# Attention on one core: one exponential over three score tiles, two score tiles ahead of each group's products, and the identity bias in 32-column array tiles

## What is computed

```python
x = x + attention(layernorm(x))
x = x + ffn(layernorm(x))
# attention, for each batch b of 4 and head h of 16
scores = q @ k.T / sqrt(8) + bias[h]      # (1024, 1024)
weights = softmax(scores)
out = weights @ v                          # (1024, 8)
out = concat(heads) @ w_gate + b_gate; a, g = split(out); return a * sigmoid(g)
```

## Time and profile before

| | us |
|---|---|
| three runs | 669.5, 670.9, 678.7 |
| median | 670.9 |
| the profiled execution | 669.6 |
| its span, first to last instruction | 667.8 |
| attention loop, first score tile to last copy | about 71 to 565 |

### The profile page before, as it was taken

One profiled execution on the slowest core, in us unless ns is written; L12 is line 12 of the kernel. 1 busy time (PEld: TensorE's weight loads), 2 busy tenths in 40 slices (PEclk: granted clock), 3 DMA queues, 4 the chain that ended last, 5 costly groups with the idle time before them and its releaser, 6 DMA issues.

```text
span 667.8 us, 12697 instructions
## 1 busy us (share of the span) xinstructions
PE 606.4 (91%) x4011; PEld 166.2 (25%) x4011; DVE 566.7 (85%) x691; ACT 548.4 (82%) x599; POOL 105.8 (16%) x95
## 2 busy tenths in 40 slices
PE   6892699999999999999999999999999998599775
PEld 2441122222222222222222222222222222234432
DVE  5973599999999999999999999999999996114776
ACT  2862599999999999999999999999999997011353
POOL 5740600010110101010110101010101101013412
PEclk8897599999999999999999999999999999855855
DMA  9136460525335261615244351615153401500004
GB/s 211 65 95 140 137 135 18 134 50 106 76 79 114 48 131 26 137 37 125 62 93 94 64 123 36 134 25 133 45 117 65 89 9 22 147 8 0 0 1 126
DMA packets 30175, 54.44 MB, mean 82 GB/s; under 512 B 9561, under 2 KB 21214, under 8 KB 29022
## 3 DMA queue, kind: packets, MB, share of 16 engines
q1 hardware_dynamic: 29870, 53.97, 36.0%
q10 hardware_dynamic: 288, 0.26, 0.1%
HBM read 43.86 MB, written 9.18 MB: 79 GB/s over the span
## 4 chain that ended last, share of the span: by engine, by line
ACT 37%; issue 31%; PE 11%; DVE 5%; DMA 3%; ACTq 1%; POOL 1%; DVEq 0%; SPq 0%
ACT pbuf L969 16%; ACT split L969 15%; PE ps L1151 4%; ACT pbuf L977 3%; PE ps L892 3%; ACT split L977 2%; PE ps L867 2%; DMA rd<-r_scratch 2%; DVE kb L1372 1%; PE ps L1153 1%; DVE split L1367 1%; PE ps L876 1%; ACTq L968 1%; PE ps L1165 1%; ACT o_sbs L733 1%
## 5 line engine op out<-in xcount | busy, mean ns | idle before, releaser
L926 DVE TENSOR_TENSOR pbuf<-ps,t 128x1024 f32<-128x1024 f32 x192 | 232.5, 1223 | 20.0 <-PE ps L867 15.4
L926 DVE TENSOR_TENSOR split<-ps,t 128x1024 f32<-128x1024 f32 x192 | 229.4, 1217 | 12.9 <-PE ps L867 7.3
L969 ACT ACTIVATE pbuf<-pbuf 128x1024 f32<-128x1024 f32 x192 | 207.2, 1260 | 19.8 <-DVE pbuf L926 19.6
L867 PE MATMUL ps<-qb,kb 64*128 64x512 f16 x1024 | 184.0, 390 | 22.1 <-SPq L793 14.8
L969 ACT ACTIVATE split<-split 128x1024 f32<-128x1024 f32 x192 | 202.5, 1268 | 1.1 <-DVE split L926 1.0
L892 PE MATMUL ps<-pbuf,vst 128*32 128x512 f32 x1024 | 137.2, 608 | 0.0
L892 PE MATMUL ps<-split,vst 128*32 128x512 f32 x1024 | 136.0, 604 | 1.0 <-ACT split L977 1.0
L867 PEld LDWEIGHTS ps<-qb,kb 64*128 64x128 f16 x1024 | 48.4, 93 | 308.7 <-DVE pbuf L926 113.9
L876 PE MATMUL ps<-t64s,ident 128*64 128x512 f16 x512 | 80.6, 395 | 0.0
L977 ACT ACTIVATE split<-ps 128x1024 f32<-128x1024 f32 x64 | 78.6, 1228 | 0.0
L977 ACT ACTIVATE pbuf<-ps 128x1024 f32<-128x1024 f32 x64 | 78.2, 1222 | 0.0
(11 more groups left out here) (134 smaller groups left out, 359.1 us busy)
## 6 DMA issues: line engine op xcount, KB each, us to landing
t<-g_scratch SPq DMA_DIRECT2D x16, 960.0 KB
kb<-k_scratch SPq DMA_DIRECT2D x120, 64.0 KB
t64s<-gh_scratch SPq DMA_DIRECT2D x16, 248.0 KB
t64s<-gl_scratch SPq DMA_DIRECT2D x16, 248.0 KB
qb<-q_scratch SPq DMA_DIRECT2D x60, 64.0 KB
x_sb<-in_L_attn_x SPq DMA_DIRECT2D x4, 512.0 KB, 7.6
q_scratch<-split SPq DMA_DIRECT2D x8, 256.0 KB, 3.4
k_scratch<-split SPq DMA_DIRECT2D x8, 256.0 KB, 3.7
```

The source lines that it names most:

```text
L867: last = eng.matmul(ps[:, u + c, :], kb[p][rows, keys], qb[p][rows, b * HALF:(b + 1) * HALF], start=True, stop=True)
L926: eng.tensor_tensor(slot(g, b), banks(unit(k), 2), t128[p][:, t * P:t * P + S], ALU.add).then_inc(z_ready, 1)
L969: eng.activation(buf, buf, ACT.Exp).then_inc(p_ready, 1)
```

## The change

It does three things in the attention loop.

- ScalarE does batches 0 to 2 of a group in a single exponential over 3072 adjacent columns (`slots`), and it does the PSUM tile of batch 3 first. A semaphore `pd_ready` of its own counts the PSUM exponentials; `p_ready` now counts the wide ones.
- TensorE issues score tiles 0 and 1 of group g + 2, then the identity products of group g + 1, then products half 0 of g, score tile 2, products half 1, score tile 3. The identity products have become a function of their own, `bias(i, g)`, and stand a group later than the scores that they add to.
- The identity products are eight matmuls with 32 output columns in place of four with 64, so they use the same shape of array tile as the products. The band is loaded 32 columns wider.

VectorE's code is not touched. ScalarE's copy of half 1 stands between the PSUM exponential and the wide one of group 1.

```diff
@@ sizes
-T64W = 2 * S - 64
+T64W = 2 * S - 32
@@ in scores: batch 3 waits for the PSUM exponential alone
-                            eng.wait_ge(p_ready, i * (8 * GPH) + 4 * g)
+                            eng.wait_ge(pd_ready, i * (2 * GPH) + g)
@@ the identity products
-                    for c in range(2):
-                        for m in range(2):
-                            c0 = t * P + 64 * m + c * HALF
-                            last = eng.matmul(ps[64 * m:64 * m + 64, u + c, :], ident2[:, :],
+                def bias(i, g):
+
+                    p, t = (g // GPH) % 2, g % GPH
+                    for c in range(2):
+                        for m in range(4):
+                            c0 = t * P + 32 * m + c * HALF
+                            last = eng.matmul(ps[32 * m:32 * m + 32, 4 + c, :], ident2[:, 0:32],
                                               t64[p][:, c0:c0 + HALF], start=False, stop=True,
                                               skip_group_check=True)
                     last.then_inc(sp_ready, 1)
@@ in products, half 0
-                        eng.wait_ge(p_ready, i * (8 * GPH) + 4 * (g + 1))
+                        eng.wait_ge(pd_ready, i * (2 * GPH) + (g + 1))
+                        eng.wait_ge(p_ready, i * (2 * GPH) + (g + 1))
@@ TensorE's list
-                        for steps, c in (((0,), 0), ((1,), 1), ((2, 3), None)):
...
-                                for b in steps:
-                                    scores(i, g + LAG, b)
...
-                            if c is not None:
-                                products(i, g, c)
+                        if g + LAG < 2 * GPH:
+                            scores(i, g + LAG, 0)
+                            scores(i, g + LAG, 1)
+                            bias(i, g + LAG - 1)
+                            products(i, g, 0)
+                            scores(i, g + LAG, 2)
+                            products(i, g, 1)
+                            scores(i, g + LAG, 3)
+                            continue
@@ ScalarE's list
-                        for b in range(B):
-                            buf = slot(g, b)
-                            if b < DPG:
-                                eng.wait_ge(z_ready, i * (2 * DPH) + (DPG * g + b + 1))
-                                eng.activation(buf, buf, ACT.Exp).then_inc(p_ready, 1)
...
-                                eng.activation(buf, banks(4, 2), ACT.Exp).then_inc(p_ready, 1)
+                        eng.wait_ge(sp_ready, i * (2 * GPH) + (g + 1))
+                        eng.wait_ge(groups_done, i * (2 * GPH) + (g + 1))
+                        eng.activation(slot(g, DPG), banks(4, 2), ACT.Exp).then_inc(pd_ready, 1)
...
+                            copy_half(eng, 0, 1).then_inc(o_ready[1], 1)
+                        eng.wait_ge(z_ready, i * (2 * DPH) + DPG * (g + 1))
+                        eng.activation(slots(g, DPG), slots(g, DPG), ACT.Exp).then_inc(p_ready, 1)
```

More of the change, by code:

```diff
@@ L725, in attention_block @@
         p_ready = sem("p_ready")
+        pd_ready = sem("pd_ready")
         GPH = TB
@@ L749, in slot, with slots @@
             return pbuf[:, n, :] if n < 8 else splitf[:, (n - 8) * S:(n - 7) * S]
+        def slots(g, n):
+            k = 4 * (g % SETS)
+            return big[:, k * S:(k + n) * S] if k < 8 else splitf[:, (k - 8) * S:(k - 8 + n) * S]
         def unit(k):
@@ L902, in _ @@
                         scores(0, g, b)
+                    if g < LAG - 1:
+                        bias(0, g)
                 with eng.Fori(0, NH2) as i:
                     for g in range(2 * GPH):
-                        for steps, c in (((0,), 0), ((1,), 1), ((2, 3), None)):
-                            if g < 2 * GPH - LAG:
-                                for b in steps:
-                                    scores(i, g + LAG, b)
[L910 to L914, removed]
-                            if c is not None:
-                                products(i, g, c)
+                        if g + LAG < 2 * GPH:
[7 more added lines that the diff above has]
+                            continue
+                        if g + LAG == 2 * GPH:
+                            with eng.If(i < NH2 - 1):
+                                scores(i, g + LAG, 0)
+                                scores(i, g + LAG, 1)
+                            bias(i, g + LAG - 1)
+                        else:
+                            with eng.If(i < NH2 - 1):
+                                scores(i, g + LAG, 0)
+                                scores(i, g + LAG, 1)
+                                bias(i, g + LAG - 1)
+                        products(i, g, 0)
+                        with eng.If(i < NH2 - 1):
+                            scores(i, g + LAG, 2)
+                        products(i, g, 1)
+                        with eng.If(i < NH2 - 1):
+                            scores(i, g + LAG, 3)
             @block.vector
@@ L964, in _ @@
                     for g in range(2 * GPH):
-                        for b in range(B):
-                            buf = slot(g, b)
-                            if b < DPG:
-                                eng.wait_ge(z_ready, i * (2 * DPH) + (DPG * g + b + 1))
-                                eng.activation(buf, buf, ACT.Exp).then_inc(p_ready, 1)
[L970 to L976, removed]
-                                eng.activation(buf, banks(4, 2), ACT.Exp).then_inc(p_ready, 1)
[L978 to L986, removed]
-                                copy_half(eng, 0, 1).then_inc(o_ready[1], 1)
@@ new lines, in _ @@
+                        if g == SETS // 2:
+                            eng.wait_ge(qk_out, 16 * 4 * B)
+                        eng.wait_ge(sp_ready, i * (2 * GPH) + (g + 1))
+                        eng.wait_ge(groups_done, i * (2 * GPH) + (g + 1))
+                        eng.activation(slot(g, DPG), banks(4, 2), ACT.Exp).then_inc(pd_ready, 1)
+                        if g == LAG - 1:
+                            with eng.If(i > 0):
+                                eng.wait_ge(groups_done, i * (2 * GPH) + SETS)
+                                eng.wait_ge(o_stored[1], i * (16 * B))
+                                copy_half(eng, 1, 1).then_inc(o_ready[1], 1)
@@ L988, in _ @@
+                        if g == GPH + LAG - 1:
+                            eng.wait_ge(groups_done, i * (2 * GPH) + (GPH + SETS))
+                            eng.wait_ge(o_stored[0], i * (16 * B) + 16 * B)
+                            copy_half(eng, 0, 1).then_inc(o_ready[1], 1)
+                        eng.wait_ge(z_ready, i * (2 * DPH) + DPG * (g + 1))
+                        eng.activation(slots(g, DPG), slots(g, DPG), ACT.Exp).then_inc(p_ready, 1)
                 eng.wait_ge(groups_done, H * GPH + SETS)
```

1 line of the change is left out of this document (removed).

## The result

The changed kernel takes 716.6 us (median of four runs, 712.6 to 718.6); the kernel before, measured beside it, 671.0. The ratio is 1.065, 95% interval 1.055 to 1.074. The forecast was 692, with a range of 683 to 705: the direction was right, the size was half of what came. The profiled execution took 717.3 with a span of 715.2, 47.4 more than before.

A forecast was written before the change was run, and what follows sets the result against it. ScalarE was taken to set the 3.75 us period, TensorE 0.02 behind. Period 3.2, head ends 17.1 and edges 1.1 and 0.7 add 22.1 to the profiled 669.6, 691.7; forecast 692, range 683 to 705.

The forecast's parts named there:

- rival A: Attention loop: engine work counts and waits hide, period falls to 3.57, 23 us less, 647; chance 5%.
- the chain over two groups: Products through identity products, PSUM and wide exponentials to products two groups later: 7.46 us, so period at least 3.73.
- score tile 1's wait for VectorE: Score tile 1 overwrites banks VectorE's third addition reads: starts at 4.05 instead of 3.95, period 3.78.
- VectorE's copy holding up two additions: Head's end: copy waits for products ahead of two additions, score tile 1 is 1.3 us late, 1.2 after slack.
- the edges: Loop's start and end: first products wait for one more addition, +1.1 us; last products come 3.57 after the previous, +0.7.
- The bias parts' loads: Head loads growing from 1984 to 2016 columns, 1.6%, under a 30 us head: priced at nothing.
- 1.14 at its end: Extra time at each of 15 head ends, from both copies' waits, less today's 0.48: +17.1 us in all.
- 0.03 in each of 8 groups: Mid-head period 3.78 against 3.75, over 128 groups: +3 to +4 us, taken as 3.2.
- gave back: Head's end: the gap after ScalarE's copy returns 0.16 us, since ScalarE is then fed early.
- B's shorter chain: No measurable change: exponential 2.58 and quicker notices, period 3.65, about 676; chance 12% including a cheaper-copies case at about 683.
- C's causes: Heavier: 32-column identity tiles run worse, or VectorE's pitch is 1.20; 5 to 14 us over forecast, 697 to 706; 13%.
- the assumption: TensorE's granted clock stays at its upper level of 1.00 in the loop; a fall at head ends wasn't excluded.

The follow-up runs named there:

- one_wait: Changed kernel without the products' wait for the PSUM exponential, leaving one semaphore: loop 532.3 us against 535.1, 31.98 to 32.08 between copies where no load is late.
- all_four_mended: Changed kernel with VectorE's copy behind the third addition, ScalarE's copy first, q loads earlier and one semaphore ahead of products: loop 495.1 us, total 672.4.
- q_loads_earlier: Changed kernel with the next head's four q loads issued ahead of the waits for the two copies: loop 523.6 us against 535.1, total 706.6.
- identity_64_columns: Changed kernel with the identity products as before, four of 64 columns: loop 532.6 us against 535.1, lowest between copies 32.23.

## Why the prediction was right and wrong

**Right, and shown.** Engine work shrank as worked out (wide exponential 2.76 for 2.77; eight identity products in two passes), and none of it arrived, for rival A's counter-argument: the chain over two groups. Its length is in the traces: no two successive periods of the loop, head's ends included, add to less than 7.55 in the changed kernel, where the prediction had 7.46. With a single semaphore ahead of the products the least is 7.46 (one_wait, all_four_mended), and with three exponentials, 2.94 for 2.76, it is 7.73. TensorE's old order makes the chain 0.2 shorter, so that it fits under TensorE's own work, and takes away score tile 1's wait for VectorE; the period falls to 3.72. VectorE's copy holding up two additions was the largest single item: moving it took 19 us off the loop, and the gap it makes was 4.99 for a forecast 4.98. At the edges the first products came 1.1 later, as forecast, and the last products came 3.56 after the ones before (600.74, 604.30), forecast 3.57.

**The step that failed most.** "The bias parts' loads grow from 1984 to 2016 columns, 1.6%, under a head that is 30 us long: nothing." The size was not the question. I compared the loads with a head's length, but they start only when both copies are done and are needed by the first score tile two groups before the head's end, which left 22.4 us in the kernel before; no row was read for how much of that they use. The change makes the copy that triggers them later and the tile that needs them earlier: 20.5 us are left between the two, 1.9 less, and the loads took up to 23.1. It cost 11.6 us of the profiled loop, shown by the q loads sent earlier and again by ScalarE's copy put first.

**Mis-sized terms.** Free of late loads, a head costs 1.81 more than before, where I had 1.14 at its end and 0.03 in each of 8 groups, 1.37 or so. Gap by gap between first products, in q_loads_earlier, the 0.44 lie behind ScalarE's copy (4.54 for 4.36) and in the five mid-head periods (3.99, 3.85, 3.71, 3.85 and 3.80, on average 3.84 in place of 3.78); the gap between the two gave back 0.05 more than forecast. One cause is shown: the start of the products after an exponential, taken from a row with one semaphore (0.05) though the diff gives them two (0.14), worth 0.27 a head by the one_wait run. Where the other 0.17 come from is open. The second half's products waiting 0.44 for ScalarE's copy are not it: with the copy put first that wait is gone, and only one gap fell, by 0.49, the copy's own slot.

**Chance.** 5.9 us of the profiled difference lie behind the loop, in the granted clock of unchanged code. What makes the clock fall there in some executions and not in others stays open. It doesn't explain the medians, which differ by 45.6. The mean granted clock was 0.907 in the profiled execution and 0.903 in q_loads_earlier, the two with some 109 us behind the loop, and 0.911 to 0.919 in the ten experiments with 102.7 to 104.6. The changed kernel's other three runs have 0.915 to 0.919 and still took 712.6, 715.9 and 718.6. With 71.1 ahead of the loop and some 103.4 behind it, an estimate from those traces, their loops took 536 to 542, more than the profiled 535.1. So the late loads probably cost more there than 11.6.

So the miss of 25.3 (47.4 less the forecast 22.1) is 11.6 of late loads, 6.6 of mis-sized terms (15 x 0.44), 5.9 behind the loop, and 1.2 that I can't place.

**The rivals.** A (the gain arrives) fell. B's shorter chain too: the exponential took 2.76, not 2.58, and the notices were slower. Of C's causes the first, 32-column tiles running worse, was tested twice and is nothing. The second, a VectorE pitch of 1.20, did occur, in two groups of a head: with the input ready an addition follows the last by 1.13 to 1.14, but where its score tile comes just before it by 1.23 or 1.30. The first of these two rows has such an addition, the second none:

```profile
281.75 3.66 DVE L952 TENSOR_TENSOR split<-ps,t 128x1024 f32<-128x1024 f32 x3 [0.90 <-PE ps L873]
...
297.22 3.49 DVE L952 TENSOR_TENSOR split<-ps,t 128x1024 f32<-128x1024 f32 x3 [0.36 <-PE ps L873]
```

No score tile waited behind either kind of late addition, so it cost nothing that shows. The loss beyond my range had another source.

Of the granted clock in the loop, the assumption held: 1.00 in every 100 us from 100 to 600, with idle pieces up to 2.6 us ahead of a head's first score tile.

## What to carry to other kernels

When an engine's list is strict, a wait that was free is priced by what stands behind it: before an instruction is moved on one engine, look for every rare instruction elsewhere (a copy once a head, a transfer's trigger) that waits for it, and for what is queued behind that one. A transfer hidden under a long stage has a start and a need of its own; read the distance between the two and how much of it is used, never the stage's length. And when work between a producer and its consumer is made coarser, add up the whole chain between them, over as many groups as it spans, and compare it with the busiest engine's own work over as many: three results handed over at once are fine where the chain stays below it (some 7.34 against 7.44) and useless where one score tile ahead of the identity products lifts it above (7.55).

## What the runs showed of the hardware

A second semaphore on the same instruction costs time even if it was reached long ago: products with two started 0.14 us after the exponential's end, with one 0.04 to 0.05. In the kernel before, a VectorE addition that also waits for a free buffer started 0.52 after its score tile's start, though a score matmul lasts 0.39; the additions that wait for their scores alone started 0.43 after. That is 0.13 against 0.04, but on VectorE no run took the second wait away.

A change of the array's shape costs about 0.10 us of TensorE: the last identity pass stood 0.22 ahead of the products in the same shape and 0.31 in another (identity_64_columns). Yet that one change more per group left the time between copies at 32.23, in a kernel in which TensorE was not the one waited for.

SyncE's queue needed 10.6 to 11.3 us to issue a head's 18 transfers, from 0.28 us for a `kb` load to 0.63 for a `qb` load. With the same issue order, the tile that waits for them started 20.5 us after the queue's first transfer in some heads and 23.1 in others of one execution. What spreads them was not tried.
